# Twelve places instead of six for the rows and results of expert tiles in a mixture-of-experts kernel on one Trainium2 core

## The reference

```python
logits = x @ gate_w.T                        # 2048 tokens, 64 experts
scores = softmax(logits)
topk_w, topk_ids = top_k(scores, 6)
topk_w = topk_w / (sum(topk_w) + 1e-20)
# every token goes through its 6 experts
g, u = split(x @ w_gate_up[e].T)             # 2 x 176 columns
routed += topk_w * ((silu(g) * u) @ w_down[e].T)
shared  = (silu(sg) * su) @ ws_down.T        # all tokens
x = x + routed + shared
```

## Time and profile before

| | us |
|---|---|
| median of 3 runs | 1591.05 (1586.62 to 1592.08) |
| the profiled execution | 1586.48, span 1584.8 |
| PE busy | 1296.5 (82%) |
| DVE busy | 782.7 (49%) |
| GpSimd busy | 501.6 (32%) |
| ACT busy | 378.4 (24%) |
| queue of SP, ACT (q1) | 170.41 MB, 40.3% of 16 engines |
| queue of GpSimd (q0) | 34.78 MB, 7.8% of 16 engines |

### The profile page before, as it was taken

How to read it: one execution, slowest core, us unless ns; L and a number is a source line. 1 busy time by engine, 2 the same in 40 slices (tenths; PEclk the granted TensorE clock), 3 DMA queues, 4 the chain that set the end, 5 groups by cost and what they waited for, 6 DMA issues and landing times. The chain is left out here.

```text
span 1584.8 us, 23113 instructions
## 1 busy us (share of the span) xinstructions
PE 1296.5 (82%) x6092; PEld 913.2 (58%) x6092; DVE 782.7 (49%) x2105; ACT 378.4 (24%) x746; POOL 501.6 (32%) x602
## 2 busy tenths in 40 slices
PE   3859999748799999976999679668888888888960
PEld 2435555436588888843555455446666666666640
DVE  6746666277613121153544357954444444444437
ACT  1205555423312111021333221112111111121110
POOL 0042222342200000001000202946666666666640
PEclk9959999888999999988999889879999999999985
DMA  3698887221000000036543202068888788888749
GB/s 110 222 181 115 122 118 113 81 66 63 28 1 1 0 0 1 0 132 205 142 130 101 74 30 59 1 195 261 257 260 243 237 251 255 254 258 248 229 138 337
DMA packets 151178, 218.57 MB, mean 138 GB/s; under 512 B 43974, under 2 KB 80826, under 8 KB 151111
## 3 DMA queue, kind: packets, MB, share of 16 engines
q1 hardware_dynamic: 123175, 170.41, 40.3%
q0 software_dynamic: 15264, 34.78, 7.8%
q10 hardware_dynamic: 12672, 12.58, 2.3%
HBM read 173.11 MB, written 52.50 MB: 142 GB/s over the span
## 5 line engine op out<-in xcount | busy, mean ns | idle before, releaser
L1713 PE MATMUL experts_ps_gu<-experts_wgu,experts_xt 128*128 128x352 f32 x636 | 218.9, 467 | 1.9 <-DMA experts_wgu<-L_ffn_w_gate_up 1.4
L701 DVE TENSOR_REDUCE att_mx<-att_ps 128x1 f32<-128x512 f32 (+3 forms) x240 | 151.7, 654 | 133.2 <-PE att_ps L568 66.5
L1840 POOL DMA_INDIRECT y_parts<-experts_y,moe_target x159 | 161.6, 1016 | 127.1 <-DVE experts_picked L1804 57.0
L564 PE MATMUL att_ps<-att_ks,att_qs 96*128 96x512 f32 (+4 forms) x384 | 157.1, 475 | 30.6 <-DMA att_ks<-k_parts 27.7
L1834 POOL DMA_INDIRECT experts_x<-x_rows,moe_source x159 | 157.2, 989 | 61.4 <-issue 41.9
L1734 PE MATMUL experts_ps_y<-experts_wd,experts_ht 96*128 96x256 f32 x636 | 167.0, 385 | 0.0
L1756 ACT ACTIVATE experts_xt<-experts_ps_x 128x256 f32<-128x256 f32 x159 | 60.9, 383 | 416.4 <-PE experts_ps_x L1702 410.9
L661 ACT ACTIVATE att_pt<-att_ps 128x1024 f32<-128x1024 f32 (+3 forms) x160 | 121.8, 765 | 133.2 <-PE att_ps L586 132.4
L1713 PEld LDWEIGHTS experts_ps_gu<-experts_wgu,experts_xt 128*128 128x128 f32 x636 | 121.6, 193 | 47.2 <-DMA experts_wgu<-L_ffn_w_gate_up 3.1
L564 PEld LDWEIGHTS att_ps<-att_ks,att_qs 96*128 96x128 f32 (+1 forms) x384 | 78.3, 207 | 94.4 <-issue 61.6
L1702 PE MATMUL experts_ps_x<-all_ident,experts_x 128*128 128x128 f32 x318 | 72.2, 309 | 66.7 <-DMA experts_x<-x_rows,moe_source 66.0
(11 more groups left out here) (213 smaller groups left out, 2080.4 us busy)
## 6 DMA issues: line engine op xcount, KB each, us to landing
experts_wgu<-L_ffn_w_gate_up SPq DMA_DIRECT2D x159, 352.0 KB, 4.1
experts_wd<-L_ffn_w_down SPq DMA_DIRECT2D x159, 176.0 KB
att_qs<-q_parts SPq DMA_DIRECT2D x112, 128.0 KB, 3.5
att_ks<-k_parts SPq DMA_DIRECT2D x112, 128.0 KB, 5.3
combine_got<-y_parts ACTq DMA_DIRECT2D x24, 512.0 KB, 8.9
q_parts<-qkv_hi SPq DMA_DIRECT2D x8, 512.0 KB, 2.9
q_parts<-qkv_lo SPq DMA_DIRECT2D x8, 512.0 KB, 3.7
k_parts<-qkv_hi SPq DMA_DIRECT2D x8, 512.0 KB, 2.9
```

The lines of the kernel that those rows point to most:

```text
L564: ins = pe.matmul(out, qs[a][z][0:rows_a, h, i * P:(i + 1) * P], ks[a][z][0:rows_a, h, 0:width(i)], start=a == 0, stop=a == last_part and ...
L701: dve.tensor_reduce(mx[:, hs[0]:hs[-1] + 1, i], ps_1[:, (u.c * ng + g) % 2, 0:len(hs) * width(i)] .rearrange("p (h w) -> p h w", h=len(hs) ...
L1713: ins = pe.matmul(ps_gu[:, u.bank, 0:2 * FE], xt[:, u.bank, k, :], wgu[u.slot][:, k, :], start=k == 0, stop=k == KD - 1)
L1840: pool.indirect_dma_start(out=parts_dram[:, :], out_offset=bass.IndirectOffsetOnAxis(ap=target[:, n:n + 1], axis=0), in_=y[n % R][:, :], i ...
```

## The change

`FLIGHT` becomes 12. Inside `experts` R is now a constant 6 and L = FLIGHT = 12. `x`, `share` and `y` and their semaphores get L places; `wgu` and `wd` and their conditions keep R. The loops' bodies hold L tiles. GpSimd issues 11 gathers ahead of the first scatter instead of 5. The bound of the scatters, PART_ROWS - 1, is put into a register once instead of at each scatter.

```diff
-FLIGHT = 6
+FLIGHT = 12
...
-    R = FLIGHT
+    R = 6
     G = 3
+    L = FLIGHT
...
-        x = [s.sbuf(f"x{z}", [P, ROW]) for z in range(R)]
+        x = [s.sbuf(f"x{z}", [P, ROW]) for z in range(L)]
...
-        share = [s.sbuf(f"share{z}", [P, 1]) for z in range(R)]
+        share = [s.sbuf(f"share{z}", [P, 1]) for z in range(L)]
...
-        y = [s.sbuf(f"y{z}", [P, D]) for z in range(R)]
+        y = [s.sbuf(f"y{z}", [P, D]) for z in range(L)]
...
-                self.n = t * R + c
+                self.n = t * L + c
                 self.slot, self.bank = c % R, c % G
-                self.turn = t + c // R
+                self.turn = t * (L // R) + c // R
+                self.flight, self.trip = c % L, t + c // L
...
-        TURNS = NTILE // R
+        TURNS = NTILE // L
...
-            for u in range(-2, R):
+            for u in range(-2, L):
                 body(Tile(0, u))
-            with eng.Fori(1, TURNS - 2) as t:
-                for c in range(R):
+            with eng.Fori(1, TURNS - 1) as t:
+                for c in range(L):
                     body(Tile(t, c))
-            for u in range((TURNS - 2) * R, NTILE + 1):
+            for u in range((TURNS - 1) * L, NTILE + 1):
                 body(Tile(0, u))
...
-            for u in range(R):
-                step(Tile(0, u), True)
+            for u in range(L):
+                step(Tile(0, u), u < R)
             with sp.Fori(1, TURNS - 1) as t:
-                for c in range(R):
+                for c in range(L):
                     step(Tile(t, c), False)
...
-                pe.wait_ge(x_loaded[u.slot], 16 * (u.turn + 1))
+                pe.wait_ge(x_loaded[u.flight], 16 * (u.trip + 1))
...
-                if u.plus(-R).exists():
-                    dve.wait_ge(y_placed[u.slot], 16 * u.turn)
+                if u.plus(-L).exists():
+                    dve.wait_ge(y_placed[u.flight], 16 * u.trip)
...
-                z = n % R
-                if n >= R:
-                    pool.wait_ge(x_turned, n - R + 1)
-                    pool.wait_ge(shared_out, n - R + 1)
+                z = n % L
+                if n >= L:
+                    pool.wait_ge(x_turned, n - L + 1)
+                    pool.wait_ge(shared_out, n - L + 1)
...
-                                        in_=y[n % R][:, :], in_offset=None, bounds_check=PART_ROWS - 1,
+                                        in_=y[n % L][:, :], in_offset=None, bounds_check=last_row,
                                         oob_is_err=False)\
-                    .then_inc(y_placed[n % R], 16)
-
-            for n in range(R - 1):
+                    .then_inc(y_placed[n % L], 16)
+
+            last_row = pool.to_reg(PART_ROWS - 1)
+            for n in range(L - 1):
                 fetch(n)
             for n in range(NTILE):
-                fetch(n + R - 1)
+                fetch(n + L - 1)
                 put(n)
```

More of the change, by code:

```diff
@@ L1612, in experts @@
         cells_loaded = [s.sem(f"cells_loaded{z}") for z in range(R // G)]
-        x_loaded = [s.sem(f"x_loaded{z}") for z in range(R)]
+        x_loaded = [s.sem(f"x_loaded{z}") for z in range(L)]
         wgu_loaded = [s.sem(f"wgu_loaded{z}") for z in range(R)]
@@ L1624, in experts @@
         y_copied = s.sem("y_copied")
-        y_placed = [s.sem(f"y_placed{z}") for z in range(R)]
+        y_placed = [s.sem(f"y_placed{z}") for z in range(L)]
         shared_out = s.sem("shared_out")
@@ L1685, in _ @@
             sp.wait_ge(cells_loaded[0], 16)
-            for u in range(R):
-                step(Tile(0, u), True)
+            for u in range(L):
+                step(Tile(0, u), u < R)
             with sp.Fori(1, TURNS - 1) as t:
-                for c in range(R):
+                for c in range(L):
                     step(Tile(t, c), False)
-            for u in range((TURNS - 1) * R, NTILE):
+            for u in range((TURNS - 1) * L, NTILE):
                 step(Tile(0, u), False, u + R - G + 1 < NTILE)
@@ L1699, in turn_x @@
                 wait(pe, xt_ready, u.n)
-                pe.wait_ge(x_loaded[u.slot], 16 * (u.turn + 1))
+                pe.wait_ge(x_loaded[u.flight], 16 * (u.trip + 1))
                 for k in range(KD):
-                    ins = pe.transpose(ps_x[:, k * P:(k + 1) * P], x[u.slot][:, k:D:KD], ident[:, :])
+                    ins = pe.transpose(ps_x[:, k * P:(k + 1) * P], x[u.flight][:, k:D:KD], ident[:, :])
                 ins.then_inc(x_turned, 1)
@@ L1793, in copy_y @@
                 dve.wait_ge(y_done, u.n + 1)
-                if u.plus(-R).exists():
-                    dve.wait_ge(y_placed[u.slot], 16 * u.turn)
-                dve.tensor_scalar(y[u.slot][:, :], ps_y[:, u.bank, 0:D], share[u.slot][:, 0:1], None, ALU.mult)\
+                if u.plus(-L).exists():
+                    dve.wait_ge(y_placed[u.flight], 16 * u.trip)
+                dve.tensor_scalar(y[u.flight][:, :], ps_y[:, u.bank, 0:D], share[u.flight][:, 0:1], None, ALU.mult)\
                     .then_inc(y_copied, 1)
@@ L1802, in take_share @@
                     return
[L1803 to L1806, removed]
+                dve.wait_ge(x_loaded[u.flight], 16 * (u.trip + 1))
+                dve.scalar_tensor_tensor(out=picked[:, :], in0=x[u.flight][:, ROW_ID:ROW_ID + TOP],
+                                         scalar=owner[:, bass.ds(u.n, 1)], in1=x[u.flight][:, ROW_W:ROW_W + TOP],
+                                         op0=ALU.is_equal, op1=ALU.mult, accum_out=share[u.flight][:, :])\
                     .then_inc(shared_out, 1)
@@ L1841, in put @@
                                         out_offset=bass.IndirectOffsetOnAxis(ap=target[:, n:n + 1], axis=0),
[L1842 removed]
+                                        in_=y[n % L][:, :], in_offset=None, bounds_check=last_row,
                                         oob_is_err=False)\
[L1844 to L1846 removed]
+                    .then_inc(y_placed[n % L], 16)
+            last_row = pool.to_reg(PART_ROWS - 1)
+            for n in range(L - 1):
                 fetch(n)
             for n in range(NTILE):
[L1849 removed]
+                fetch(n + L - 1)
                 put(n)
[L1851 to L1852 removed]
+            for z in range(L):
+                pool.wait_ge(y_placed[z], 16 * ((NTILE - 1 - z) // L + 1))
 def add_parts(nc, tag, x_sb, parts_dram, y_dram):
```

## The result

The changed kernel takes 1529.38 us in the median of 4 runs (1526.0 to 1531.25), the kernel before 1591.57 in 4 runs (1586.62 to 1596.77). The ratio is 0.9607, 95% interval 0.9571 to 0.9642: 62 us less. The prediction said 1530, between 1505 and 1562.

The account below looks back on a forecast made before the run. Late row gathers, in a loop through latency, bound the experts stage. After the change, 134 steps at 2.70 plus 22 at 2.60 make 419.0 us against 477.0, 58.0 less: 1528.5, said as 1530, range 1505 to 1562 us.

Parts of the forecast that it names:

- The late party: Experts stage: gathered rows come late through a latency loop of 9.77 us over three tiles; some 0.55 us a tile is waiting.
- DMA-bound, 2.62 to 2.78 a tile: Experts stage after the change: the DMA engines set the pace, taken as 2.70 us a tile; chance 0.42.
- The 134 heavy steps: Experts-stage tile steps before about 1460 us, whose scatters still carry rows: priced at 2.70 us each, 361.8 us.
- the favourable 2.58: Experts stage: us a tile for full DMA engines at the packet times seen between 1100 and 1460 us.
- The 22 light steps: Experts-stage tile steps from about 1460 us, whose scatters carry nothing: priced at GpSimd's 2.60 us each, 57.2 us.
- the signs in the profile: Expected afterwards: row waits near zero, turns 2.6 to 2.75 us apart, DMA share 0.95 or more, a weight load late.
- It stays covered: Weight loads in the experts stage: issued 10.4 us ahead of use against 6.0 us of landing, so not late.
- rival 1: Experts stage: GpSimd or the Tensor engine sets the pace, DMA does not; 1515, 1510 or 1501 us; chance 0.27.
- rival 2: Experts stage: unevenly loaded DMA engines give only 266 GB/s, 2.92 us a heavy tile; 1558 us; chance 0.20.
- rival 4: GpSimd's gather issue lengthens from 0.95 to 1.96 us with more gathers outstanding; slower, 1668 us; chance 0.06.
- The move hides in that gap: GpSimd's register move before each scatter hides in the 0.30 us gap; removing it was counted as 0, at most 4.6 us.
- The start and the doubled loops: Six more gathers before the first scatter: 0, at worst 3 us; loop bodies twice as long: 0, other end 24 us.

Follow-up runs that it names:

- leads 5, 6 and 8: The changed kernel with gathers five, six or eight tiles ahead of the scatter instead of eleven: 1567.46, 1526.38 and 1529.14 us.

## Why the prediction was right, point by point

The late party. Gathers were late, by a loop through latency; with more lead the waits for rows (148.7 us of DVE) went to none, and the gain came in the stage and nowhere else. Shown by leads 5, 6 and 8.

The new limit. "DMA-bound, 2.62 to 2.78 a tile": measured 2.656 over the stage, at a share of 0.97. Shown by the run with fewer bytes. The two kinds of tile can be told apart by the turn of tile 136:

```profile
1409.71 0.40 PE L1704 MATMUL experts_ps_x<-all_ident,experts_x 128*128 128x128 f32 x2
```

The 134 heavy steps were priced at 2.70 and took 2.649: 6.9 us less. I had set the bounds from packets that take longer with a backlog (281/0.97 = 290 GB/s for full engines) or not (300). The packets did not slow down: 293/0.97 = 302. What kept the step above the favourable 2.58 is that the engines reached a share of 0.97, not 1. The 22 light steps were priced at 2.60 and took 2.699: 2.2 us more. There my rate of 281 for a lighter mixture was too good (253 from 1400 to 1440; 683/253 = 2.70), and GpSimd's 2.60, which I took as the floor, isn't one. The errors partly cancel: 419.0 forecast, 414.3 measured.

That 1530 and 1529.38 agree to a microsecond is luck in part. The stage gave 4.7 us more than forecast and the rest 1.0, and the profiled execution gave 5.5 back by starting the stage later. And the signs in the profile were not all as I had them: the turns do not lie 2.6 to 2.75 us apart, more than half of them keep the Tensor engine's 2.51 and the others wait longer.

Weights. "It stays covered" did not hold. A wgu load landed in 7.8 us instead of the 6.0 that I used, still less than the 10.4 ahead of its use, yet for some tiles weights were late (above). The same section had the Tensor engine without any wait for weights before; there is a line of 1.0 us. More places would not have helped, as the run with twelve showed, since full engines deliver no more. The list of signs, with a weight load as the new late party, had this right.

GpSimd as a floor (rival 1). Wrong as a mechanism: I had worked out that its lead covers the 0.09 us a tile for a long while, and still charged 2.60. Over the whole stage the cover holds, even at 2.529 a tile.

Unevenness between engines (rival 2). The best 20 us windows of before, 266 to 269 GB/s, were no ceiling. They were bounded by the loop, not by the engines; the sustained rate after is 293. The Trainium skill ("DMA: Bandwidth & Descriptors", "Issuing engines are not separate DMA queues") has all issuers on the same 16 engines, and the runs agree: gathers from GpSimd landed in 6.5 us, and in 4.7 when only SyncE's weights had fewer bytes. Its limit of about 358 GB/s in "Where 436 GB/s comes from" is not what held this mixture at 293.

GpSimd's issue with many gathers (rival 4). The changed kernel's slow issues are the third and the fourth gather, before it was the fourth and the fifth; all seven behind them take 0.94 to 0.95 us with more of them outstanding:

```profile
1050.22 1.97 POOL L1836 DMA_INDIRECT experts_x<-x_rows,moe_source  x1 [0.30 <-issue]
...
1052.49 0.94 POOL L1836 DMA_INDIRECT experts_x<-x_rows,moe_source  x1 [0.30 <-issue]
```

The run with twelve places for weights separates the two explanations. Its twelve memsets of wd instead of six put the vector additions off, and the slow issues move with them: the first five gathers take 0.94 to 1.19 us, and it is the sixth and the seventh that are slow.

```profile
1045.45 4.63 DVE L1822 TENSOR_TENSOR all_x<-all_x,moe_shared 128x1024 f32<-128x1024 f32 x4
...
1046.03 1.47 POOL L1834 DMA_INDIRECT experts_x<-x_rows,moe_source  x1 [0.30 <-issue]
...
1047.80 1.97 POOL L1834 DMA_INDIRECT experts_x<-x_rows,moe_source  x1 [0.30 <-issue]
```

So it is the additions beside them, not the number in flight.

The register. This step failed, though it left the sum whole. "The move hides in that gap" was read from scatters that had y already. The ones that mattered waited for y. One of them was on the table too, the put at 1303.51, but I did not look how far it lay behind its copy, and 0.81 us went into the loop as latency that nothing could change. Alone, the register is worth 27 us; beside a longer lead nothing, since the loop that it shortens no longer binds (1532.04 without it against 1529.38 with it, and there a waiting scatter still starts 0.80 us after its copy). The reason that the total was right is that both parts of the change relieve the same loop, and the sum was made from the floors above it, not by adding up the parts.

The start and the doubled loops. No cost is to be seen: from the first gather to the turn of tile 2 are 9.6 us, 9.8 before.

## What to carry to other kernels

When a loop through latency is the limit, price the change from the next floors (each engine's busy time for a step; for DMA the bytes by the packet times seen, at a share that a backlog reaches, 0.97 here), not from the parts of the loop; and look for the smallest lead that passes the crossing, here one tile, 41 us, where the other five bought nothing. On GpSimd's queue put nothing between a wait and the indirect DMA that it guards, not even a register move, where the loop that it stands in is the limit: compute bounds ahead of the wait. A queue that is slower than the pace by a few per cent is no floor as long as its lead and its places last to the end of the stage.

## What the runs showed of the hardware

A 29 ns register move on GpSimd's queue between a semaphore wait and an indirect DMA put the DMA's start 0.53 us later (0.81 instead of 0.28 us after the end of the releasing instruction); the same move ahead of the wait cost nothing (0.29). A mixture of weight loads (2 to 2.8 KB rows), gathers and scatters (about 1 KB rows) ran at 293 GB/s with a DMA share of 0.97 for 300 us, where plain transfers reach 384. An indirect DMA's issue took up to 1.97 us instead of 0.95 beside vector additions with both inputs in SBUF. Rows left out of a gather by its bound save their DMA time: 44 KB a tile less, some 7.5 us in all.
